# A graph attention block on one core: x by rows and transposed, edge lists laid out, the gate's first layer in the main loop, loads on two queues, and the norm by square root and reciprocal

## The reference

```python
xn = layernorm(x)
# 1: graph attention, 4 heads of 64
h = xn @ W
a_src, a_dst = (h * att_src).sum(d), (h * att_dst).sum(d)   # per head
e = leaky_relu(a_src[src] + a_dst[dst], 0.2)
alpha = segment_softmax(e, dst)
g = sigmoid(segment_sum(alpha * h[src], dst) + bias)
# 2: linear attention with a gate, 8 heads
q, k, v = xn @ Wqkv;  context = softmax(k, over nodes)^T v
xm = layernorm(xn) * ln_g + ln_b
gate = sigmoid(gelu(xm @ Wg1 + bg1) @ Wg2 + bg2)            # 256 -> 64 -> 256, exact gelu
m = (q context) * gate @ Wproj + bproj
x = x + g + m
# 3: feed-forward on the chosen half of the nodes
xn2 = layernorm(x);  weights = xn2 @ wr
y = gelu(xn2 @ w1 + b1) @ w2 + b2                           # 256 -> 1024 -> 256, tanh gelu
x = x + where(in_top_half(weights), y * weights, 0) + xn2
```

## Time and profile before

| | |
|---|---|
| median of 3 runs | 1323.71 us (1321.82 to 1324.46) |
| profiled execution | span 1323.1 us |
| TensorE busy | 1060.3 us, 80% |
| VectorE busy | 1018.3 us, 77% |
| ScalarE busy | 516.7 us, 39% |
| GpSimd busy | 854.3 us, 65%, of it 816.0 in 832 gathers |
| moved by DMA | 212 MB, mean 160 GB/s; 269 GB/s in the first fortieth |

### The profile page before, as it was taken

How to read it: one execution, slowest core, us unless ns; L and a number is a source line. 1 busy time by engine, 2 the same in 40 slices (tenths; PEclk the granted TensorE clock), 3 DMA queues, 4 the chain that set the end, 5 groups by cost and what they waited for, 6 DMA issues and landing times.

```text
span 1323.1 us, 24146 instructions
## 1 busy us (share of the span) xinstructions
PE 1060.3 (80%) x5817; PEld 791.9 (60%) x5817; DVE 1018.3 (77%) x2596; ACT 516.7 (39%) x1155; POOL 854.3 (65%) x891
## 2 busy tenths in 40 slices
PE   5998857785687878878788787897877978779786
PEld 4674635553465566656666566675665766567565
DVE  6776365657788877888788887888878878888788
ACT  4462423212334434343353443434434334344421
POOL 0621656767777777777777777777777777777000
PEclk9999878886788889888898888988889888898889
DMA  9527556766666666666666666666666666665205
GB/s 269 136 72 141 155 184 179 191 178 166 161 173 166 164 160 165 176 158 166 169 162 174 165 161 176 158 171 164 164 173 161 168 164 166 175 164 151 68 1 195
DMA packets 165907, 212.04 MB, mean 160 GB/s; under 512 B 49524, under 2 KB 131252, under 8 KB 165704
## 3 DMA queue, kind: packets, MB, share of 16 engines
q0 software_dynamic: 39984, 110.94, 33.8%
q1 hardware_dynamic: 117570, 97.15, 25.6%
q10 hardware_dynamic: 8306, 3.41, 1.2%
HBM read 165.93 MB, written 45.46 MB: 160 GB/s over the span
## 4 chain that ended last, share of the span: by engine, by line
PE 50%; DVE 15%; issue 11%; ACT 7%; DMA 3%; SPq 1%; DVEq 1%; ACTq 0%; POOL 0%; POOLq 0%
PE bank L1922 15%; PE bank L1887 14%; PE bank L1859 6%; PE bank L1898 5%; ACT L1630 4%; PE bank L1838 3%; DVE hot L1272 2%; PE bank L1847 2%; PE bank L2009 2%; PE bank L1738 2%; DVE ring L1357 2%; DVE xnT L1552 1%; DVE late L1394 1%; DMA parts_d<-wout 1%; ACT bn L1630 1%
## 5 line engine op out<-in xcount | busy, mean ns | idle before, releaser
L774 POOL DMA_INDIRECT ring<-feat_d,idx x832 | 816.0, 981 | 285.8 <-issue 226.5
L1357 DVE TENSOR_TENSOR ring<-ring,bank 128x1024 f32<-128x1024 f32 x208 | 240.0, 1217 | 1.8 <-ACT bank L1620 1.8
L1922 PE MATMUL bank<-late,w_s 128*128 128x256 f32 x768 | 232.4, 463 | 0.4 <-ACT hT L1680 0.4
L1887 PE MATMUL bank<-ring,hot 128*64 128x265 f32 x1664 | 206.8, 401 | 13.3 <-DVE ring L1357 13.2
L1922 PEld LDWEIGHTS bank<-late,w_s 128*128 128x128 f32 x768 | 183.6, 243 | 36.0 <-ACT hT L1680 0.5
L1887 PEld LDWEIGHTS bank<-ring,hot 128*64 128x64 f32 x1664 | 120.0, 141 | 93.8 <-issue 34.2
L1859 PE MATMUL bank<-w_s,hT 128*128 128x256 f32 x720 | 171.0, 392 | 1.2 <-ACT hT L1705 1.2
L1838 PE MATMUL bank<-ident,lk 128*16 128x128 f32 x208 | 42.7, 345 | 161.3 <-DVE lk L1317 161.3
L1620 ACT ACTIVATE bank<-diff 128x64 f32<-128x64 f32 x52 | 11.8, 228 | 376.5 <-DVE diff L1341 362.4
L1859 PEld LDWEIGHTS bank<-w_s,hT 128*128 128x128 f32 x720 | 137.7, 196 | 20.9 <-ACT hT L1705 1.4
L1838 PEld LDWEIGHTS bank<-ident,lk 128*16 128x16 f32 x208 | 17.5, 103 | 177.8 <-DVE lk L1317 136.8
(11 more groups left out here) (284 smaller groups left out, 1611.0 us busy)
## 6 DMA issues: line engine op xcount, KB each, us to landing
parts_d<-zero SPq DMA_DIRECT2D x59, 265.0 KB, 4.0
parts_d<-wout SPq DMA_DIRECT2D x208, 66.2 KB
lists<-dloc_d SPq DMA_DIRECT2D x104, 128.0 KB
ring<-feat_d,idx POOLq DMA_INDIRECT x832
parts<-parts_d SPq DMA_DIRECT2D x49, 265.0 KB
big<-in_x SPq DMA_DIRECT2D x7, 896.0 KB, 11.1
three<-in_x SPq DMA_DIRECT2D x49, 128.0 KB, 3.0
out<-xnT SPq DMA_DIRECT2D x5, 896.0 KB, 4.2
```

The source lines that it names most:

```text
L774: pool.indirect_dma_start(out=ring[:, u * TI + q, 0:AW], out_offset=None, in_=feat_d, in_offset=bass.IndirectOffsetOnAxis(ap=idx[:, u, q:q ...
L1357: V.tensor_tensor(feats, feats, ex[:, g * TG:(g + 1) * TG, :].unsqueeze(3) .to_broadcast([P, TG, HEADS, HD]), ALU.mult).then_inc(S("scaled ...
L1887: mm = T.matmul(bank[2 + n][c * WIN:(c + 1) * WIN, 0:SW], hot[:, q, :], ring[:, u * TI + q, 0:SW], start=(j == 0), stop=(j == TG - 1))
L1922: mm = T.matmul(bank[6 + g][:, m % 2 * 2 * P:(m % 2 + 1) * 2 * P], w1_s[:, t, m * P:(m + 1) * P], xn2T[:, t, :], start=(t == 0), stop=(t = ...
```

## The change

- The host's layout now passes x twice, by rows (partition-major) and transposed, and passes the edge lists in the layouts in which they are used, as floats, with the next target beside each; sources come as ready indices. The transposes of x and of the lists, their copies, and GpSimd's passes over the lists go. The first four parts of both x are issued by ScalarE's queue, the others by SP's.
- The feature product has 264 columns. It uses four banks in turn; keys are computed beside every second product. VectorE evacuates only the features, ScalarE copies the target scores. Statistics and roots come in four lots.
- The gate's first layer is computed in the main loop: TensorE `hidden_ahead` (4 instructions, L1772), one step ahead of use; VectorE `scale_hidden` (L1204) multiplies by the inverse standard deviation, which SP loads as a broadcast row from a small DRAM table (`load_scales`, before the window writes) in place of the hidden tile; ScalarE `gate_hidden` takes the exact gelu (L1609).
- The inverse root is Sqrt on ScalarE (L1589) and a reciprocal on VectorE (L1338). `root_table` is a square root of a constant, ahead of the copies of the sums; nothing reads its result.

The core of the diff:

```diff
-WA = C + 2 * HEADS + GH
+WA = C + 2 * HEADS
...
+                    part = slice(n * XC, (n + 1) * XC)
+                    sp.dma_start(xnT[:, part, :], xt[:, part, :]).then_inc(S(f"x{n}_in"), 16)
+                    sp.dma_start(big[:, part, :], x[:, part, :]).then_inc(S(f"x{n}_in"), 16)
...
+                for p in range(PAIRS):
+                    store(p)
+                    if p < 2:
+                        load_x(BY_SCALAR + 1 + p)
+                    if p == 2:
+                        sp.wait_ge(S("pool_made"), 7)
+                    if 2 <= p < CLEARED + 3:
+                        clear(NT if p == 2 else p - 3)
...
+                for n in range(BY_SCALAR):
+                    part = slice(n * XC, (n + 1) * XC)
+                    act.dma_start(xnT[:, part, :], xt[:, part, :]).then_inc(S(f"x{n}_in"), 16)
+                    act.dma_start(big[:, part, :], x[:, part, :]).then_inc(S(f"x{n}_in"), 16)
+                act.wait_ge(S("pool_made"), 5)
+                A.activation(spare[:, 0, 0:1], epsc[:, 0:1], ACT.Sqrt)
...
                 def evacuate(i):
-                    products = bank[2 + i % 2]
                     dve.wait_ge(S("feat_done"), i + 1)
                     if i >= 2 * SLOTS:
                         dve.wait_ge(S(f"feat_out{i // 2 % SLOTS}"), 16 * (i // (2 * SLOTS)))
-                    V.tensor_scalar(feat_pair[i // 2 % SLOTS][:, i % 2, :], products[:, 0:AW], rstd[:, i:i + 1], None, ALU.mult
+                    V.tensor_scalar(feat_pair[i // 2 % SLOTS][:, i % 2, :], prod_bank(i)[:, 0:AW], rstd[:, i:i + 1], None, ALU.mult
                                     ).then_inc(S("feat_made"), 1)
...
+                    j = key_beside(i - 1) if i else None
+                    if j is not None:
+                        dve.wait_ge(S("keys_kept"), j + 1)
+                        if j:
+                            dve.wait_ge(S("key_max"), j)
+                        V.tensor_tensor(rmax[:, :], rmax[:, :], big[:, j, :], ALU.max).then_inc(S("key_max"), 1)
...
                 def body(i):
-                    act.wait_ge(S("hid_asked"), i + 1)
-                    if i >= 2:
-                        act.wait_ge(S("hid_turned"), i - 1)
-                    A.activation(sd[:, i % 2, 0:GH], sc[:, i % 2, 0:GH], ACT.Gelu).then_inc(S("hid_made"), 1)
...
+                    act.wait_ge(S("feat_made"), i + 1)
+                    A.activation(adst_s[:, i, :], prod_bank(i)[:, AW:AW + HEADS], ACT.Copy, scale=rstd[:, i:i + 1]
+                                 ).then_inc(S("adst_made"), 1)
+                    j = key_beside(i)
+                    if j is not None:
+                        act.wait_ge(S("keys_done"), j + 1)
+                        A.activation(big[:, j, :], bank[4 + j % 2][:, 0:C], ACT.Identity, bias=padneg[:, j:j + 1],
+                                     scale=rstd[:, j:j + 1]).then_inc(S("keys_kept"), 1)
...
+                def products(i):
+                    pe.wait_ge(S(f"x{i // XC}_in"), 32)
+                    if i >= 4:
+                        pe.wait_ge(S("adst_made"), i - 3)
                     for t in range(CT):
-                        mm = T.matmul(bank[2 + u][:, 0:WA], tile[:, t * P:(t + 1) * P], wa_s[:, t, :],
+                        mm = T.matmul(prod_bank(i)[:, 0:WA], xnT[:, i, t * P:(t + 1) * P], wa_s[:, t, :],
                                       start=(t == 0), stop=(t == CT - 1))
                     mm.then_inc(S("feat_done"), 1)
-                    if i < EARLY:
-                        if i >= 2:
-                            pe.wait_ge(S("keys_kept"), i - 1)
+                    j = key_beside(i)
+                    if j is not None:
+                        if j == 0:
+                            pe.wait_ge(S("weights_ready"), 4)
+                        if j >= 2:
+                            pe.wait_ge(S("keys_kept"), j - 1)
                         for t in range(CT):
-                            mm = T.matmul(bank[4 + u][:, 0:C], tile[:, t * P:(t + 1) * P], wk_s[:, t, :],
+                            mm = T.matmul(bank[4 + j % 2][:, 0:C], xnT[:, j, t * P:(t + 1) * P], wk_s[:, t, :],
                                           start=(t == 0), stop=(t == CT - 1))
                         mm.then_inc(S("keys_done"), 1)
...
-                    sp.dma_start(hidT[:, u, :], hid_d[bass.ds(i, 1), :, :].rearrange("a b c -> (a b) c")
+                def load_scales(i, u):
+
+                    if not known_below(i, 2):
+                        sp.wait_ge(S("hidT_made"), i - 1)
+                    sp.dma_start(rrow[:, u, :], rstd_d[bass.ds(i, 1), :].to_broadcast([GH, P])
+                                 ).then_inc(S(f"scales_in{u}"), 16)
...
+                def scale_hidden(i, u):
+                    dve.wait_ge(S("sums_kept"), NB * (i + LAG_MERGE - 1) + 1)
+                    scale_hidden_from(hid_ps[0], i, u)
+
+                def scale_hidden_from(hid, i, u):
+                    dve.wait_ge(S("hid_done"), i + 1)
+                    dve.wait_ge(S(f"scales_in{u}"), 8 * (i - u) + 16)
+                    V.tensor_tensor(rrow[:, u, :], hid, rrow[:, u, :], ALU.mult).then_inc(S("hid_scaled"), 1)
...
+                def inverse(i, u):
+                    dve.wait_ge(S("root_made"), PRO_ROOTS + i + 1)
+                    V.reciprocal(bn[:, u, 9:10], bn[:, u, 8:9]).then_inc(S("inverted"), 1)
+
                 def normed(i, u):
-                    dve.wait_ge(S("root_steps"), 2 * i + 2)
+                    inverse(i, u)
+                    dve.wait_ge(S("inverted"), i + 1)
                     if u == 0 and not known_below(i, 2):
...
-                def inverse_root(i, u):
+                def root(i, u):
 
                     act.wait_ge(S("var_made"), i + 1)
-                    A.activation(bn[:, u, 8:9], bn[:, u, 7:8], ACT.Ln, bias=epsc[:, 0:1]).then_inc(S("root_steps"), 1)
-                    act.wait_ge(S("root_steps"), 2 * i + 1)
-                    A.activation(bn[:, u, 9:10], bn[:, u, 8:9], ACT.Exp, scale=-0.5).then_inc(S("root_steps"), 1)
...
+                    A.activation(bn[:, u, 8:9], bn[:, u, 7:8], ACT.Sqrt, bias=epsc[:, 0:1]).then_inc(S("root_made"), 1)
+
+                def root_table(i, u):
+                    A.activation(spare[:, u, 0:1], epsc[:, 0:1], ACT.Sqrt)
...
+                def gate_hidden(i, u):
+                    act.wait_ge(S("hid_scaled"), i + 1)
+                    if not known_below(i, 2):
+                        act.wait_ge(S("gate_done"), i - 1)
+                    A.activation(hidT[:, u, :], rrow[:, u, :], ACT.Gelu, bias=b1col[:, 0:1]).then_inc(S("hidT_made"), 1)
...
-                steps(act, [EDGES(exps), MERGE(merge_exp), HALF(hidden), LOAD_MIXER(load_mixer), MAXIMUM(logarithms), CONTEXT(context), EDGES(keep_sums),
-                            SUM(inverse_root), MERGE(gates), TURN(keep_turned)])
+                steps(act, [EDGES(exps), MERGE(merge_exp), HALF(hidden), MERGE(gate_hidden), LOAD_MIXER(load_mixer), MAXIMUM(logarithms), CONTEXT(context), SUM(root_table), EDGES(keep_sums),
+                            SUM(root), MERGE(gates), TURN(keep_turned)])
...
+                def hidden_ahead(i, u):
+                    pe.wait_ge(S("sums_kept"), NB * (i + LAG_MERGE - 2) + 1)
+                    if not known_below(i, 1):
+                        pe.wait_ge(S("hid_scaled"), i)
+                    hidden_to(hid_ps[0], i)
+                def hidden_to(hid, i):
+                    for t in range(CT):
+                        mm = T.matmul(hid, wg1_s[:, t, :],
+                                      xnT[:, bass.ds(i, 1), t * P:(t + 1) * P].rearrange("p a c -> p (a c)"),
+                                      start=(t == 0), stop=(t == CT - 1))
+                    mm.then_inc(S("hid_done"), 1)
...
-                           EDGES(first_sums), EDGES(other_sums), AHEAD(scores_ahead), MAXIMUM(maximum), PREPARE(prepare), CONTEXT(context),
+                           NODE_AHEAD(hidden_ahead), EDGES(first_sums), (NI - 1, NI, last_hidden), EDGES(other_sums), AHEAD(scores_ahead), MAXIMUM(maximum), PREPARE(prepare), CONTEXT(context),
```

564 lines of the change are left out of this document (250 added, 314 removed).

## The result

| | before | after |
|---|---|---|
| median | 1322.76 us (1318.36 to 1324.46, 4 runs) | 1301.13 us (1295.7 to 1304.13, 4 runs) |
| profiled execution, span | 1323.1 us | 1299.1 us |
| prologue, to the first list load | 136.8 us | 110.4 us |
| context phase, to the eighth fill | 162.9 us | 160.5 us |
| 45 steps of the loop | 924.9 us, 20.55 a step | 928.8 us, 20.64 a step |

The ratio is 0.984 (95% interval 0.982 to 0.9861). The forecast was 1269 with a range from 1248 to 1296, so the time lies outside. The four stretches give -26.4, -2.3, +3.9 and +0.9 us, together the 24 us between the spans. The prologue gave 26 us of 44, and the loop took 4 where it was to give 8.

A forecast was written before the change was run, and what follows sets the result against it. GpSimd was taken to fill the main loop, with an equally long engines' chain, and TensorE to be busiest in the prologue. 1323.7 - 44 (prologue) - 8 (loop) - 2 (context) - 1 (tail) = 1268.7, say 1269 us; range 1248 to 1296.

The forecast's parts named there:

- What bounds the kernel now: Whole kernel: TensorE busy 111.33 of 136.80 us in the prologue; main loop GpSimd full, engines' chain equally long, 20.56 us a step.
- What goes and what comes in the loop: Main loop: norm starts 0.85 us earlier, added gate work stays off the chain; engines' chain 19.7 us a step from 20.5.
- rival 4: Main loop: ScalarE and SP slip, the node's load comes late every step; slower than before, 1326 us and more; chance 0.03.
- What takes over: Main loop: GpSimd's 16 gathers set the pace at 20.4 us a step, 8 us gained over 45 steps.
- small stretches: Main loop: minor lengthening of gathers apart from the reversed scan, put at 0.1 to 0.15 us a step.
- The scan's term: Main loop: one gather a step meets the reversed scan's last 0.2 to 0.3 us and may lose that much.
- Prologue, the start: Prologue: first feature product at 13 us, bounds 10 and 19, with 6 us for W to load.
- Prologue, the factor: Prologue: TensorE's 66 us of work times 1.12 for waits between engines, 74 us; bounds 66 and 86.
- Prologue, the end: Prologue: 6.4 us from the last evacuation to the main part's first list load, as before.
- Rest: Context phase 2 us gained (0 to 6) by larger x pieces; tail 1 us gained (-2 to 3).
- Rival 3: Prologue held by its loads and queues: 28 us gained instead of 44, 1285 us; chance 0.17.
- rival 2: Main loop: a gather meets the whole reversed scan, 21.0 us a step, 20 us lost, 1297 us; chance 0.14.

The follow-up runs named there:

- the second profile: The changed kernel profiled once more, nothing altered: main part began at 109.5 us, the 45 steps took 926.1 us, 20.58 each.

## Why the prediction was wrong, step by step

- **What bounds the kernel now**: right in its result, two chains of equal length; one gather fewer in either kernel shows it. The reason given, that GpSimd is full, does not carry it: part of that fullness was the held eighth gather.
- **What goes and what comes in the loop**: right in kind. The norm's wait went, ScalarE's order came as drawn, the node's load was not late (rival 4 did not occur), and the engines' chain is 19.4 us for 19.7 worked out.
- **What takes over**: the mechanism was right, GpSimd, and a term was mis-sized: 16 gathers at 20.38 us were to be 20.0 + 0.25 (scan) + 0.1 to 0.15 (small stretches). Measured: 20.0 + 0.29 + 0.33 = 20.62 of the 20.64. The term that failed is the small stretches. The kernel before showed it: its mean of 977 ns already stands 0.5 us a step above the floor, and the small stretches, 0.23 there, come from operations that the change does not remove. The loop is 12 of the 32 us by which the forecast was off (9 by the second profile).
- **The scan's term**: near in size, but partly by luck. It was worked out from one fixed phase, and what was left of the scan was taken as the loss. In the very step of the earlier trace rows the gather in question, at 430.94 us with 0.24 us of the scan left, took 1.00 us, only 0.05 longer. And in the changed kernel the phase does not stay: 25 of 45 scans hold a gather, the fifth or the sixth, for anything from 0.04 to 0.97 us.
- **Prologue, the start**: 13 us forecast, 18.2 measured, in its bounds. The term that failed was 6 us until W is there: W did land 5.6 us after its issue, but the second attention row, on which the same work waits, took 10.8 us, beside x on the same DMA engines.
- **Prologue, the factor**: 74 us by 1.12 times TensorE's 66, measured 83.3, factor 1.26, in its bounds too. This is the largest miss, 9 us, and the step that failed is the factor: it was carried over from the old order and lowered. The 83.3 us consist of 66 us of matmuls, 9 of waits (bias column 3.1, the rest mostly slots behind the stores) and 8 at less than the full rate: the slow start, and a granted clock of 0.88 up to 62.5 us, when TensorE had stood waiting. The prediction counted x's second copy for the start only, and put the stores, lists and clears on the same engines at nothing. The old factor, 1.15, belonged to another order: its transposes began before the weights were there, and by 62.5 us it had moved 13 MB where the new one moves 21 (210 and 333 GB/s). That this is why the factor rose is argued.
- **Prologue, the end**: 8.9 us from the last evacuation to the first list load for 6.4. SP waited 5.1 us for the last stores of features. What held them, perhaps the small rows of the target scores issued just ahead, was not tried.
- **Rest**: the tail was to give 1 us and took 0.9; the context phase gave the 2 us forecast.
- **Rival 3** (loads and queues, 28 us gained) is what happened in the prologue, **rival 2** in part in the loop. Each was given 0.14 to 0.17 by itself; that both could be half true at once, 1301, had no place in the range. All three terms of the prologue came out above their values, two of them near their upper bounds. A shared cause, the DMA engines, would explain that, but was not isolated. (Rival 4's price was also added wrongly: 1323.7 - 44 - 3 + 54 is 1331, not 1326; nothing rests on it.)
